# Attention scores as four 32-column products in place of one 128-column product

## The reference, cut to what matters

```
s   = einsum('bhtd,bhsd->bhts', q, k)
s   = s - s.mean(-1);  mad = abs(s).mean(-1) + 1e-6
s   = where(causal, s / mad * score_gain, -1000)
r   = maximum(s, 0) ** 4
att = r / (r.sum(-1) + 1e-6)
y   = einsum('bhts,bhsd->bhtd', att, v)
```

## Time and profile before

| what | value |
|---|---|
| median of 3 runs | 506.7 us (506.18 to 507.11) |
| span of the profiled execution, first to last instruction | 505.4 us |
| mean granted TensorE clock | 0.966 |
| PE busy | 441.9 us (87% of the span) |
| DVE busy | 402.7 us (80%) |
| ACT busy | 342.0 us (68%) |
| POOL busy | 243.8 us (48%) |

### The profile page before, as it was taken

How to read it: one execution, slowest core, us unless ns; L and a number is a source line. 1 busy time by engine, 2 the same in 40 slices (tenths; PEclk the granted TensorE clock), 3 DMA queues, 4 the chain that set the end, 5 groups by cost and what they waited for, 6 DMA issues and landing times. The chain is left out here.

```text
span 505.4 us, 8943 instructions
## 1 busy us (share of the span) xinstructions
PE 441.9 (87%) x2736; PEld 168.3 (33%) x2736; DVE 402.7 (80%) x832; ACT 342.0 (68%) x576; POOL 243.8 (48%) x180
## 2 busy tenths in 40 slices
PE   0879999664799999999999999999999995879996
PEld 0323444431232332333333322323323354334442
DVE  5884556976898998999989899989988969784443
ACT  3413223554999999999999999999989931523221
POOL 5940000333777686776877677676876720000000
PEclk9979999975999999999999999999999998799999
DMA  4300000025714205105114124043002300000001
GB/s 118 75 1 0 1 0 0 6 65 127 208 33 78 60 1 95 43 1 93 42 30 71 34 51 84 0 72 63 0 0 50 85 12 0 1 1 0 21 21 42
DMA packets 17796, 21.32 MB, mean 42 GB/s; under 512 B 4748, under 2 KB 10476, under 8 KB 17772
## 3 DMA queue, kind: packets, MB, share of 16 engines
q1 hardware_dynamic: 17452, 20.95, 19.2%
q10 hardware_dynamic: 320, 0.07, 0.1%
HBM read 13.02 MB, written 7.86 MB: 41 GB/s over the span
## 5 line engine op out<-in xcount | busy, mean ns | idle before, releaser
L1206 POOL TENSOR_TENSOR arena<-arena 128x1024 f32<-128x1024 f32 (+1 forms) x120 | 204.0, 1722 | 63.7 <-ACT arena L1178 63.5
L1136 DVE SCALAR_TENSOR_TENSOR arena<-bank,masks 128x1024 f32<-128x1024 f32 (+1 forms) x160 | 174.9, 1114 | 28.9 <-PE bank L1048 28.6
L1178 ACT ACTIVATE arena<-arena 128x1024 f32<-128x1024 f32 (+1 forms) x160 | 148.5, 961 | 8.8 <-DVE arena L1136 5.8
L1048 PE MATMUL bank<-Q,K 128*128 128x512 bf16 (+3 forms) x384 | 91.4, 334 | 10.6 <-DMA K<-k_parts 9.2
L1048 PE MATMUL bank<-K,Q 128*128 128x512 bf16 (+3 forms) x384 | 90.4, 331 | 11.6 <-DVE arena L1136 11.5
L1144 DVE TENSOR_SCALAR_CACHE_REDUCE bank<-bank 128x128 f32<-128x128 f32 (+7 forms) x128 | 94.8, 772 | 0.0
L1168 ACT ACTIVATE bank<-bank 128x128 f32<-128x128 f32 (+7 forms) x128 | 80.9, 632 | 8.9 <-PE bank L1048 8.6
L1079 PE MATMUL bank<-arena,Vq 128*32 128x512 f32 (+3 forms) x768 | 79.6, 495 | 0.0
L588 ACT ACTIVATE arena<-bank 128x512 f32<-128x512 f32 x40 | 23.9, 597 | 76.5 <-PE bank L463 76.5
L689 DVE TENSOR_TENSOR arena<-arena,bank 128x512 f32<-128x512 f32 x40 | 27.4, 686 | 42.8 <-PE bank L467 42.7
L1079 PE MATMUL bank<-arena,ones_rows 128*32 128x512 f32 (+3 forms) x640 | 61.1, 473 | 0.0
(11 more groups left out here) (122 smaller groups left out, 355.4 us busy)
## 6 DMA issues: line engine op xcount, KB each, us to landing
Q<-q_parts SPq DMA_DIRECT2D x24, 192.0 KB
att<-arena SPq DMA_DIRECT2D x28, 128.0 KB, 2.0
K<-k_parts SPq DMA_DIRECT2D x16, 128.0 KB
K<-k_parts SPq DMA_DIRECT2D x8, 192.0 KB
X<-in_L_attn_x SPq DMA_DIRECT2D x4, 256.0 KB, 4.6
K<-k_parts SPq DMA_DIRECT2D x16, 64.0 KB
out_x<-X SPq DMA_DIRECT2D x4, 256.0 KB, 2.3
q_parts<-arena SPq DMA_DIRECT2D x3, 256.0 KB
```

Of the source, the lines that this page charges most:

```text
L1048: last = nc.tensor.matmul(bank[:, lo + shift:hi + shift], left[par][:, g, blk * P:(blk + 1) * P], right[par][:, g, s0:s0 + hi - lo], start ...
L1136: nc.vector.scalar_tensor_tensor(Y(r, g)[:, lo - off(r):hi - off(r)], tiles[slot["lower", r, g]][:, lo:hi], 0.0, mask, ALU.max, ALU.mult). ...
L1178: nc.scalar.activation(z, Y(r, g)[:, tile_low(r) - off(r):T - off(r)], ACT.Square)\
L1206: nc.gpsimd.tensor_tensor(z, z, z, ALU.mult).then_inc(fourth_p, 1)
```

## The change

In `fill` each score product with 128 stationary columns becomes four with 32 stationary columns, columns j to j + 31 for j = 0, 32, 64, 96. Each streams the same moving columns and writes 32 of the 128 PSUM partitions. The values are the same. Nothing else is touched: order, waits, tiles and the semaphore, which is raised by the last product of a fill, stand as before. PE gets 768 x 4 = 3072 score products and as many weight loads in place of 768.

```diff
                     for lo, hi in bank_pieces(col, col + width(blk)):
                         s0 = seq + lo - col
-                        last = nc.tensor.matmul(bank[:, lo + shift:hi + shift], left[par][:, g, blk * P:(blk + 1) * P],
-                                                right[par][:, g, s0:s0 + hi - lo], start=True, stop=True)
+                        for j in range(0, P, 32):
+
+                            last = nc.tensor.matmul(bank[j:j + 32, lo + shift:hi + shift],
+                                                    left[par][:, g, blk * P + j:blk * P + j + 32],
+                                                    right[par][:, g, s0:s0 + hi - lo], start=True, stop=True)
                 last.then_inc(lower_ready if kind == "lower" else upper_ready, 1)
```

## The result

| | before | changed |
|---|---|---|
| median, us | 506.75 (506.18 to 507.11, 4 runs) | 511.47 (508.68 to 640.32, 4 runs) |
| ratio | | 1.008, 95% interval 1.0045 to 1.0116 |
| span of the profiled execution, us | 505.4 | 506.8 |

The forecast was 497.2 us, 493.5 to 505. One of the four runs took 640.32 us with a mean granted clock of 0.658.

A forecast was written before the change was run, and what follows sets the result against it. The attention stage was taken as bound by a chain from PE to DVE to ACT and back, ACT having most work. Seven periods at 1.3 us plus 0.4 gave 9.5 us, so 506.7 - 9.5 = 497.2 us, range 493.5 to 505.

The forecast's parts named there:

- part (4): PE's longer loop in the attention stage: two jumps back might wait for code, 0 to 3.8 us in all; taken as nothing.
- a lower clock: Attention stage: given no separate case, since PE's waits would not come near the length of the first load's wait.
- Part (1): Attention stage: all products share the 32-column form, so 17 score-sum trips a period lose their price, 4.1 us of PE.
- The trip's 0.24 us: Extra PE time going from score products to sums and back in attention: 1.54 us measured against 1.30 within one form.
- The change doesn't do what it says: Rival: the trip's price lies in switching bf16 to float32 and back, so nothing is gained, 506.7 us; chance 0.07.
- Part (2): Four score products for one in attention: stream side by side, with instruction supply costing PE 0.9 us a period.
- the rival of a slow supply: PE's sequencer hands out pairs at 55 ns in attention; about 1 us a period slower, near 515 us; chance 0.11.
- The sum of the gain: Attention stage: 1.3 us a period over seven periods, 9.1 us, plus 0.4 for the first quad: 9.5 us.
- bounded a period at 34.05 us: Attention period if all ACT's waits go: 1.25 us, plus 0.3 at most from earlier starts, so 1.55 us less.
- the 0.25 us that I held back: Attention period: a few ACT waits left because pieces bunch, so 1.3 us taken of the 1.55 us bound.
- The first quad: First attention quad, with no earlier quad's sums and a wait for its load: given 0.4 us of gain.
- the 12.4 that I took for the bound: Largest gain in attention: 8 x 1.55 us, giving 494.3 us; below that ACT would need shorter instructions.

The follow-up runs named there:

- the run with the quads written out: The changed kernel with PE's eight quads written out one after the other, so no loop and no jump back: 492.89 us, ratio 0.9725.
- rounds 0 and 4: The changed kernel with four 32-column products only in rounds 0 and 4, full products in the others, loop kept as written: 498.18 us, ratio 0.984.
- twos: The changed kernel with each score product as two of 64 stationary columns in place of four of 32, with the loop: 508.49 us, ratio 1.0025.
- rounds 0, 1 and 4: The changed kernel with four 32-column products only in rounds 0, 1 and 4, full products elsewhere, same loop: 509.28 us, ratio 1.0022.
- rounds 0, 1, 2 and 4: The changed kernel with four 32-column products only in rounds 0, 1, 2 and 4, full products elsewhere, same loop: 501.43 us, ratio 0.99.
- quarters: The kernel before, with each score product over 128 columns issued as four over a quarter of the moving columns, 128 stationary columns each: 518.52 us, ratio 1.0223.
- the shifted run: The changed kernel with full products in the first quad's rounds 1 and 4, shortening PE's program ahead of the untouched loop: 503.43 us, ratio 0.9936.
- the repeat: The changed kernel measured once more with nothing altered, ten runs: 508.98 us, ratio 1.0028.

## Why the prediction was wrong

**The step that failed is part (4),** "I take nothing: the trace shows no such wait, and a packet's fetch is far below a period", with its bound of 3.8 us in all. I had the mechanism (the loop may no longer stay, two jumps back), but priced it as one DMA of 16 KB, 1.9 us, and put it at zero. The branch alone took 3.59 and 3.34 us: 0.9 to 1.0 before the packet moves, 1.2 and 0.9 for its moving, and 1.4 and 1.6 from there to PE's next instruction. A second fetch soon behind it was no term of the sum at all. In the profiled execution the first stops are 3.16 and 2.86 us, the second ones 1.16 and 3.89: 11.0 us of PE. Against the run with the quads written out (492.89 us) the changed kernel lost 16 us (508.98, ten runs) to 19 us (511.47). More than PE's stops is lost because PE's late tiles stop DVE and ACT, and because the clock fell. The two turns tell these apart roughly, against periods of 33.93 us: the first, at full clock, lost 5.0 us (37.05 + 35.80 - 67.86) with 4.3 us of stops; the second, with 10.24 us at a clock of 0.50, lost 10.3 (36.75 + 41.45 - 67.86) with 6.75 us of stops. The prediction had said that a lower clock is no case of its own, since PE's waits would not come near the first load's; it took the waits from a trace without these stops.

PE's loop, counted from branch to branch in the trace with its sequencer's own instructions (a few records can be missing), is kept at 1,181 (before), 1,461 (rounds 0 and 4) and 1,565 (twos), and not kept at 1,751 (rounds 0, 1 and 4), 2,041 (rounds 0, 1, 2 and 4), 2,141 (quarters) and 2,333 (the change). The Trainium skill's page "Runtime: NRT & Kernel Launch" (section "Instruction fetch mechanics") has the rule that speaks against this change: code is fetched in sequence, in blocks of 256 instructions, and a taken branch whose target is no longer held stalls until it is fetched. The runs agree with the stall (a branch of 3.3 to 3.9 us in place of 0.2). On the size they don't: the page speaks of a window of two such blocks, and a loop of 1,565 was kept; it also gives PE room for 2,048 instructions, and a loop of 1,751 was already too long.

**Part (1) was right,** and so was the path by which it gains: in periods without a jump ACT is busy nearly all the time (33.73 of 33.93 us). The trip's 0.24 us is the price of changing the array form, and it goes when the forms are equal, though the products still go from bf16 to float32 and back; it stays with 64 columns. "The change doesn't do what it says" is refuted.

**Part (2) was too dear.** I took 0.9 us a period for the supply. The timeline of PE in the changed kernel has a whole fill of 384, 512 and 128 columns, and the start of the next:

```profile
234.58 0.61 PE L1050 MATMUL bank<-Q,K 128*32 128x384 bf16 x12
235.02 0.34 PE L1050 MATMUL bank<-K,Q 128*32 128x384 bf16 x4
```

Its twelve pairs take 0.44 us, and the streaming of 1,024 columns needs 0.43 (0.16 + 0.22 + 0.05). So next to nothing is lost, and the rival of a slow supply (55 ns a pair, 515 us) is refuted by the run with the quads written out. The kernel did come out on that rival's side, by another mechanism.

**The sum of the gain was too small.** I bounded a period at 34.05 us and forecast 34.3; it is 33.93 in the run with the quads written out. ACT's idle time fell by 1.34 us a period (1.54 to 0.20), where the list of waits had let me bound it at 1.25, and its busy time fell by 0.33 (34.06 to 33.73), where I had 0.3 at most. So both went to their bounds and a little past, and the 0.25 us that I held back for waits that stay were not needed. The first quad, for which I took 0.4 us, gave 35.05 - 33.40 = 1.65. In sum 13.9 us (506.77 - 492.89) for 9.5 forecast, and more than the 12.4 that I took for the bound.

**What stays open.** How many instructions are kept exactly, between 1,565 and 1,751 here, and whether it depends on where the loop starts in its packets. Why a branch takes 3.3 us or more when its packet moves in about 1.2; SP issues loads of the next quad in the same stretch, and no run moved them away. What the clock costs by itself, since it falls behind some jumps and not behind others. And the run of 640 us.

## What to carry to other kernels

Products of one array form in a row cost PE little more than their streaming in this kernel; each way there and back between two forms cost 0.24 us here, so let small and large products share a form where they alternate. But count the instructions that the edit adds inside a loop: when a loop's program no longer stays, each jump back can cost microseconds, as it did here, and it shows in the page as more instruction packets and in the waits as "issue" of PE. Writing the loop out (code then came in sequence, and hidden) turned this change from 0.3 to 0.8% slower into 2.75% faster.

## What the runs showed of the hardware

- A jump back to code that is not held stopped PE for 2.7 to 3.4 us (the branch itself took 3.3 to 3.9 us, and 0.2 where the loop was kept). Where only 51 to 83 recorded instructions stood between the target and the next packet, it stopped PE a second time, mostly for 1.2 to 3.9 us. Code in sequence, 38 packets in the written-out run, stopped PE for no more than 0.2 us; in the shifted run one such stop of 0.64 us stands.
- Four 32-column bf16 products side by side have the pace of one 128-column product at 384 and 512 columns, weight loads included (mean load 97 ns, and 98 before).
- The granted clock of the changed kernel fell to 0.50 for 10.24 us in the middle of the stage, after PE had stood still for 2.86 us and worked again for 0.94 us. Behind the first jump, with a stop of 3.16 us, it did not fall (in the repeat it did, from 225.06 to 228.48); in the written-out run, without stops, it stayed at 1.00 from 124.5 to 391 us.
